# Denominators as jobs on a ring of three PSUM banks, Z in the staging tile, and the first batch's maxima and masks moved out of the opening pass

## What is computed

```python
xn = layernorm(x)
# A: 8 heads, latent attention; 32 latent dims each for queries, keys and a shared key part
c_q, c_kv, k_r = xn @ W_DQ + b_DQ, xn @ W_DKV + b_DKV, xn @ W_KR + b_KR
q = [c_q @ W_UQ + b_UQ, c_q @ W_QR + b_QR];  k = [c_kv @ W_UK + b_UK, k_r]
a = softmax(q @ k.T / sqrt(160)) @ (c_kv @ W_UV + b_UV) @ W_O + b_O
# B: 16 heads of 16 dims; every token's similarity to a guide vector, scaled by the
# minimum and maximum over ALL batches, gives pos = sim > 0.9; queries attend to keys of
# their own class and to 5 register keys; the 5 register queries see both classes
b = masked_attention(xn @ W_qkv, pos) @ W_proj + b_proj
out = x + a + b
```

## Time and profile before

| | us |
|---|---|
| median of three runs | 3077.69 |
| the profiled execution | 3083.09 |
| its span on the core | 3081.3 |
| PE busy (matmul) | 2900.2, 94% |
| DVE busy | 2256.7, 73% |
| ACT busy | 1676.5, 54% |
| POOL busy | 1428.3, 46% |

### The profile page before, as it was taken

The page is one execution under the profiler, slowest core; times in us unless marked ns, Lnnn a source line. Parts: engine busy times, 40 slices in busy tenths (PEclk is TensorE's granted clock), DMA queues, the critical chain, the costliest instruction groups (busy, mean ns, idle before and its releaser), DMA issues.

```text
span 3081.3 us, 45461 instructions
## 1 busy us (share of the span) xinstructions
PE 2900.2 (94%) x16898; PEld 1283.4 (42%) x16898; DVE 2256.7 (73%) x4085; ACT 1676.5 (54%) x1947; POOL 1428.3 (46%) x680
## 2 busy tenths in 40 slices
PE   5889999999999999999999999999999999999997
PEld 4634334443344443444334433444434443344433
DVE  5776787767877787767777677777787678776791
ACT  2424565544655566545565456555565456654574
POOL 6649522682227712285225832178122962258301
PEclk9979999998999999999999999999999999999998
DMA  4505234400352024411254003430145112540001
GB/s 148 180 16 98 69 86 99 82 16 30 105 100 62 19 74 97 107 27 34 68 110 89 16 31 92 102 74 20 53 101 114 31 37 63 117 92 16 17 17 36
DMA packets 128485, 211.43 MB, mean 69 GB/s; under 512 B 47560, under 2 KB 76136, under 8 KB 128120
## 3 DMA queue, kind: packets, MB, share of 16 engines
q1 hardware_dynamic: 124160, 201.10, 27.4%
q10 hardware_dynamic: 4104, 7.42, 0.6%
HBM read 136.21 MB, written 71.97 MB: 68 GB/s over the span
## 4 chain that ended last, share of the span: by engine, by line
PE 72%; DVE 13%; DMA 5%; POOL 4%; issue 3%; ACT 1%; SPq 1%; ACTq 0%; POOLq 0%; DVEq 0%
PE O L1207 20%; PE M L1108 12%; PE M L1102 10%; DVE mx L1448 10%; PE S L1192 7%; PE S L1195 6%; PE M L1128 3%; PE M L1172 2%; PE M L1174 2%; PE M L1221 2%; PE M L1140 2%; POOL PTx L734 2%; PE M L1146 1%; DMA recb_d<-RC 1%; DMA RB<-recb_d 1%
## 5 line engine op out<-in xcount | busy, mean ns | idle before, releaser
L1448 DVE TENSOR_REDUCE mx<-M 128x1 f32<-128x512 f32 x3072 | 1972.4, 683 | 567.9 <-PE M L1108 311.2
L956 ACT ACTIVATE PT<-S 128x1024 f32<-128x1024 f32 x1280 | 1241.9, 1022 | 818.5 <-PE S L1195 514.6
L1108 PE MATMUL M<-KB,QB 50*128 50x512 f32 x2048 | 671.3, 480 | 49.2 <-ACT stg L993 14.3
L1108 PEld LDWEIGHTS M<-KB,QB 50*128 50x128 f32 x2048 | 279.9, 185 | 691.6 <-DVE mx L1448 428.4
L1207 PE MATMUL O<-PT,VB 128*32 128x512 f32 x4096 | 554.6, 613 | 0.8 <-ACT PT L956 0.7
L1102 PE MATMUL M<-KA,QA 98*128 98x512 f32 x1024 | 433.0, 469 | 27.1 <-DVE mx L1448 22.0
L1195 PE MATMUL S<-QB,KB 52*128 52x512 f32 x2048 | 380.2, 434 | 6.2 <-DMA QB<-sh_d 2.3
L956 ACT ACTIVATE PTx<-S 128x1024 f32<-128x1024 f32 x256 | 250.2, 1023 | 228.2 <-PE S L1192 218.5
L1102 PEld LDWEIGHTS M<-KA,QA 98*128 98x128 f32 x1024 | 175.6, 191 | 348.8 <-DVE mx L1448 171.4
L1192 PE MATMUL S<-QA,KA 114*128 114x512 f32 x1024 | 316.0, 410 | 0.6 <-DMA QA<-sh_d 0.6
L788 POOL TENSOR_TENSOR PT<-PT,PTx 128x2048 f32<-128x2048 f32 x64 | 292.4, 4568 | 24.0 <-POOL PT L788 13.2
(11 more groups left out here) (153 smaller groups left out, 2120.0 us busy)
## 6 DMA issues: line engine op xcount, KB each, us to landing
qk_d<-stg SPq DMA_DIRECT2D x32, 1024.0 KB
KA<-kt_d SPq DMA_DIRECT2D x48, 512.0 KB, 7.3
QB<-qk_d SPq DMA_DIRECT2D x192, 128.0 KB
KB<-qk_d SPq DMA_DIRECT2D x192, 128.0 KB
kt_d<-stg SPq DMA_DIRECT2D x16, 1024.0 KB
RB<-recb_d SPq DMA_DIRECT2D x64, 256.0 KB
PT<-in_x SPq DMA_DIRECT2D x8, 1024.0 KB, 5.5
RB<-rec_d SPq DMA_DIRECT2D x32, 256.0 KB
```

Source lines behind the costliest of these rows:

```text
L956: nc.scalar.activation(probs(kind, of_a)[:, 2 * pair:2 * pair + 2, :], Sg[pair][:, :].rearrange("p (j s) -> p j s", j=2), ACT.Exp, scale=S ...
L1108: done = mm(m[:, :], QB[rows, 2 * q + a, at:at + P], KB[rows, 2 * q + a, keys], start=True, stop=True)
L1448: v.tensor_reduce(mx[:, g % 2, unit, kh:kh + 1], m[:, :], AX.X, ALU.max).then_inc(free, 1)
```

## The change

- `denominators`, `take_dens` and the semaphores of DN go. Job `dn` takes the same place in PE's order (first after `values` at steps 6, 10, ... 30 of A and step 2 of B), but writes to the next bank of the ring, each quad by itself. DVE copies the even quad's bank to half a tile in SBUF (latT, 128 x 512) and adds the odd quad's bank to it. SP stores from there.
- The ring has three banks in all of A and B.
- Z moves from PTx's memory to the staging tile `stg`. From batch 1 on POOL clears it at the head of A's stage, once the last fill of the batch is stored, and SP copies the register queries in during A's first group, after `load_b(n, 3)`. For batch 0 both stay in B's first group. The clearing grows from 1152 to 2048 columns.
- Fill `kb` (A's bias rows) goes. Its 8 rows are computed as 8 more latent columns: `Wlat` has 104 columns, made once at the start by three small matmuls, and `cq` is split and stored with 104 rows. `kt0` moves from B's step 18 to 20, `kt1` from 28 to 26.
- Opening pass: only the maxima of A's group 0 stay in it. Those of group 1 go to the first steps of batch 0's A, which now carries 160 units in 32 steps (7 a step, then 5, then 4 to 6). The extremes over partitions are found with a transpose, a DVE maximum and two small DMAs, in place of POOL's reduction. They, the marks and the masks' transposes are jobs of A's steps 1 to 6. POOL's fills of KA and KB and ACT's eight DMAs go. SP loads the selector rows and the ones from DRAM, and waits once for a DRAM to DRAM copy of them before it loads x of batch 2.

```diff
-FILLS = ("cq", "kt0", "kb", "kt1", "qk0", "qk1", "qk2", "qk3")
+FILLS = ("cq", "kt0", "kt1", "qk0", "qk1", "qk2", "qk3")
@@ prep_jobs
-    ma = max_units("a", 0) + max_units("a", 1)
-    out = [[] for _ in range(4 * B + 2)]
+    ma = max_units("a", 0)
+    out = [[] for _ in range(4 * B)]
     out[9] = [("va", 0)]
-    out[11] = fill_jobs("kb")
-    out[15] = fill_jobs("kt1")
-    for i in range(15):
-        out[17 + i] = ma[2 * i:2 * i + 2]
-    out[4 * B] = ma[30:32] + [("fa", "a", 0)] + ma[32:42]
-    out[4 * B + 1] = ma[42:]
+    out[11] = fill_jobs("kt1")
+    for i in range(16):
+        out[15 + i] += ma[2 * i:2 * i + 2]
+    out[31] += [("fa", "a", 0)]
+FIRST_MAXIMA = (7,) * 4 + (5,) * 12 + (4,) * 2 + (6, 4, 4, 6, 4, 4, 6, 4, 4, 4, 6, 4, 4, 4)
@@ jobs_b
+    s[2][2].insert(0, ("dn", QUADS - 1))
@@ jobs_a
     if first:
+        s[1][1].append(("ext",))
+        s[6][1].append(("mask",))
+    for i in range(QUADS - 1):
+        s[4 * i + 6][2].insert(0, ("dn", i))
@@
-def banks(slots, three):
+def banks(slots):
+    return [(j, 3) for step in slots for part in step for j in part]
@@ sync: a_steps, b_steps
                     if g == 0:
                         freed(b, 3)
                         load_b(n, 3)
+                        load_z(n)
...
                 if g == 0:
-                    load_z(b)
+                    if b == 0:
+                        load_z(b)
@@ gpsimd
         def clear_z(b):
-            wait_apart(pool, dn_done, b * QUADS + QUADS)
-            nc.gpsimd.memset(Z[:, 0:2 * QB_ * 144].bitcast(F32), 0.0).then_inc(z_clear, 1)
+            wait_apart(pool, st_out, stored(b, NF))
+            nc.gpsimd.memset(Z.bitcast(F32), 0.0).then_inc(z_clear, 1)
         def a_steps(n, b, before):
+            if before:
+                clear_z(n)
@@ scalar: exps
-                    act.wait_ge(dn_done, n * QUADS + i)
+                    spot = dn_spot(n, i - 1)
+                    act.wait_ge(m_full[spot.bank], spot.upto())
@@ tensor: job
+            elif kind == "dn":
+                pe.wait_ge(summed, n * ADDS + 3 * (j[1] + 1))
+                for jj in range(4):
+                    done = mm(m[32 * jj:32 * jj + 32, :], ones32[:, :], probs("a", 4 * j[1])[:, jj, :],
+                              start=True, stop=True, skip_group_check=True)
@@ vector: job
+            elif kind == "dn":
+                g, odd = j[1] // 2, j[1] % 2
+                to = DN[:, g % 2, :]
+                if odd:
+                    even = dn_spot(n, j[1] - 1)
+                    dve.wait_ge(m_free[even.bank], even.upto())
+                    v.tensor_tensor(to, m[:, :], to, ALU.add).then_inc(free, 1)
+                else:
+                    if g >= 2:
+                        dve.wait_ge(den_out, (n * GROUPS + g - 1) * 16)
+                    v.tensor_copy(to, m[:, :]).then_inc(free, 1)
             elif kind == "rs":
+                    dve.wait_ge(den_out, (n * GROUPS + GA) * 16)
```

More of the change, by code:

```diff
@@ L90, in place, with place_first @@
             step[2] = [u2, u3] + step[2]
+FIRST_MAXIMA = (7,) * 4 + (5,) * 12 + (4,) * 2 + (6, 4, 4, 6, 4, 4, 6, 4, 4, 4, 6, 4, 4, 4)
+def place_first(s):
+    units = iter(max_units("a", 1) + max_units("a", 2) + max_units("a", 3) + max_units("b", 0) + max_units("b", 1))
+    for step, n in zip(s, FIRST_MAXIMA):
+        us = list(itertools.islice(units, n))
+        front = 3 if n == 7 else 2
+        if us[0][0] == "ma":
+            step[0] += us[0:1]
+            step[2] = us[front:front + 1] + step[1] + step[2] + us[front + 1:]
+            step[1] = us[1:front]
+        else:
+            step[2] = us[n - 2:] + step[1] + step[2]
+            step[1] = us[0:n - 2]
 def jobs_b(more):
@@ L135, in jobs_a @@
             s[at][1].append(("po", 4 + c))
-    for g in range(GA):
+    if first:
+        place_first(s)
+    for g in (() if first else range(GA)):
         if g + 2 < GA:
@@ L140, in jobs_a @@
             place(s, g * NC, "b", g + 2 - GA)
-    return s
-def banks(slots, three):
-    out = []
-    for k, step in enumerate(slots):
-        out += [(j, 3 if three is not None and k >= three else 2) for part in step for j in part]
-    return out
+    for i in range(QUADS - 1):
+        s[4 * i + 6][2].insert(0, ("dn", i))
+    return s
+def banks(slots):
+    return [(j, 3) for step in slots for part in step for j in part]
 def index(jobs, used=(0, 0, 0)):
@@ L335, in program @@
     mask_f = take(2 * P).rearrange("p (s c) -> p s c", s=2)
-    one_row = take(S)
     zero = take(16)
     NH = B * NC * HB
-    n2, dots, root, newton = [take(NH) for _ in range(4)]
+    n2, dots, root = [take(NH) for _ in range(3)]
+    newton = take(NC * HB)
     xnT2 = take(2 * KD * S).rearrange("p (i k s) -> p i k s", i=2, k=KD)
@@ L641, in a_steps @@
                 kind, nxt = ("a", g + 1) if g + 1 < GA else ("b", 0)
+                if not before and g == 0:
+                    leave_extremes()
                 shift(n, kind, nxt, a_spot(n, b, ("fa", kind, nxt)))
@@ L1109, in job @@
                               start=True, stop=True)
+            elif kind == "ext":
+                pe.wait_ge(ext_ready, 1)
+                done = nc.tensor.transpose(m[0:2, 0:P], small[:, 0:2], ident[:, :])
+            elif kind == "mask":
+                pe.wait_ge(mask_ready, 1)
+                for f in range(2):
+                    done = nc.tensor.transpose(m[:, f * P:(f + 1) * P], masks[:, f, :, :].rearrange("p w c -> p (w c)"),
+                                               ident[:, :])
             elif kind == "fa":
@@ L1122, in job @@
                 pe.wait_ge(m_free[lat.bank], lat.upto())
[L1123 to L1124 removed]
+                lhs = Gk[:, 4 * int(kind[2]):4 * int(kind[2]) + 4, :].rearrange("p h i -> p (h i)")
+                done = mm(m[:, :], lhs, latT[0:LAT + 1, hf * HALF:(hf + 1) * HALF], start=True, stop=True)
             elif kind[:2] == "qk":
@@ L1209, in values @@
             last.then_inc(pv_done, 1)
-        def denominators(n, b, i):
-            g, c = i // 2, i % 2
-            if c == 0:
-                if g == 0 and b is not None:
-                    pe.wait_ge(m_free[2], b * LOOP[2] + U_B[2])
-                elif not (g == 0 and b is None):
-                    pe.wait_ge(dn_free, n * GA + g)
-            pe.wait_ge(summed, n * ADDS + 3 * (i + 1))
-            for jj in range(4):
-                last = mm(DN[32 * jj:32 * jj + 32, :], ones32[:, :], probs("a", 4 * i)[:, jj, :],
-                          start=(c == 0), stop=(c == 1), skip_group_check=True)
-            last.then_inc(dn_done, 1)
         def of_batch(j, n, b):
-            own = j[0] in ("mb", "rs", "rt", "rv", "po") or (j[0] == "fa" and j[1] == "b")
+            own = j[0] in ("mb", "dn", "rs", "rt", "rv", "po") or (j[0] == "fa" and j[1] == "b")
             return b if own else n
@@ L1272, in a_steps @@
                     values(b, STEPS_B - 1, "b")
-                if k >= 6 and k % 4 == 2:
-                    denominators(n, b, (k - 6) // 4)
                 some(k, 2)
@@ L1558, in a_steps @@
             for k in range(STEPS_A):
+                if not before and k == 5:
+                    marks()
                 for j in (j for part in slots[k] for j in part):
```

240 lines of the change are left out of this document (121 added, 119 removed).

## The result

The changed kernel takes **2926.69 us** (median of four runs, 2925.61 to 2931.60), the kernel before 3079.61 us beside it (four runs): a ratio of 0.951, 95% interval 0.949 to 0.954. The forecast was 2930. The profiled execution took 2925.61, and its span is 2923.8 us, against 3081.3.

What follows compares the result with a forecast made beforehand. PE, stalled 11.9 us by bank waits, was taken to bound A, DVE to pace B, and DVE's reductions to delay the opening's tail. 3083.1 - 36 + 3 - 51 - 40 - 28 = 2931; predicted 2930, range 2890 to 2995.

Steps and rivals of the forecast that it cites:

- part 1: A, batches 1 to 7: three banks shorten each stage from 129.8 to 122.5 us, 51 us in all (17 to 83).
- part 2: B's first group, eight batches: Z loaded a stage earlier and three banks gain 5.0 us each, 40 in all (16 to 56).
- a margin for POOL's last sum: B's first group: allowance for POOL's last addition, taking the group's estimate from 26.2 to 28.2 us.
- part 3: B's fourth group, seven batches: dropping kb gains 4.0 us each, 28 in all (7 to 33).
- part 4: Opening pass: fills and DMA issues go (7 us), extremes found sooner; A's first scores come 37 us earlier, 36 taken.
- part 5: Batch 0's A: 32 more units against bank waits saved give 147.6 us, 3 more than before (bounds 135 and 160).
- Three engines above 85% don't interleave without loss: Batch 0's A: reason for placing it at 147.6 us, with PE at 137, DVE 125.5 and POOL 120.9.
- (a): Rival: POOL takes PE's place in A, A stays near 127 and B begins 2 us late: 2979 us; chance 0.2.
- (b): Rival: only stops named by own rows (Z, kb, opening) go, banks bring little, A 127.3: 2988 us; chance 0.08.
- (e): Rival: PE's 0.60 between units is the row groups' price, not a bank wait, A stays at 129: 2996 us; chance 0.04.
- (c): Rival: cold stretches all vanish and A reaches its PE time of 118 to 119: 2893 us; chance 0.12.
- (d): Rival: POOL's additions hold DVE's 64 new denominator evictions 3.1 us each, making the kernel slower: 3129 us; chance 0.03.

Runs made afterwards that it cites:

- experiment 4: Changed kernel with GpSimd's additions over the first 256 of 512 columns only (and 1e-20 added in the even quads' copy): 2900.83 us, ratio 0.943.
- experiment 1: Changed kernel with two banks in A, not three (denominators stay jobs, B keeps three): 3038.87 us, ratio 0.988.
- experiment 9: Changed kernel with the last quad's denominators in B's step 3 in place of step 2: 2912.04 us, ratio 0.947.
- experiment 2: Changed kernel with two banks in B's steps 0 to 3 only: 2934.12 us, ratio 0.954.
- experiment 10: Changed kernel with SyncE's order edited in batch 0's A, Z cleared and loaded in B's first group, last quad's denominators in B's step 3: 2933.05 us, ratio 0.953.
- experiment 5: Kernel before the change with kt1's two jobs one step later (steps 29 and 30): 3059.59 us, ratio 0.994.
- Experiment 6: Changed kernel with a GpSimd fill of 32 partitions x 8192 put back between its first two normalisations: 2929.24 us, ratio 0.952.
- experiment 7: Changed kernel, SyncE in batch 0's A sending group 0's denominators and group 2's shift ahead of load_b(0, 1): 2913.55 us, ratio 0.948.
- run 16: Not a follow-up run: part of "PE had run 16 small ones", meaning PE had executed 16 small matmuls there; no time of its own.
- experiment 12: The kernel of experiment 10 with kt0's jobs back in B's step 18: 2940.39 us, ratio 0.955.
- experiment 3: Changed kernel with Z cleared and loaded in B's first group for all batches, in place of A's: 2921.99 us, ratio 0.950.

## Why the prediction came out right, and where its steps didn't

**What bounds A** (part 1) was read right and priced low. The 11.9 us of bank waits were all of it: PE alone is 118.0 (experiment 4) against 117.9, and the 32 pairs whose late starts made up 7.9 of them now lose 0.5. The step that failed is the placement at 122.5, "between PE's 118 and today's". I had added 4.6 us for POOL's chain and for quads of uneven length; it is 1.0. DVE was put too high as well, 97.8 us busy with eight denominators, where seven lie in A and it is 93.9. POOL's list ended even later than I had it (1010.9 - 882.4 = 128.5 us after the start, not 124; the pauses of 0.27 between additions, 16 of them, are 4.3 of that), and PE wants the last sum 8.6 us into B, so that POOL's floor for A is 128.5 - 8.6 = 120: A at 119.0 and PE's hold of 1.14 in B sit on it. Two limits 1 to 2 us apart, and the stage costs no more than the larger one: 3.5 x 7 = 24.5 us of error come from this one margin. The other side of the same sum is in experiment 1: the third bank is worth 15.9, of which the denominators as jobs eat 5.1 (I had counted their PE time as unchanged and left out that they queue).

**The clearing of Z** was expected at nothing, and is nothing: 0.95 us, with POOL idle for 8.83 ahead of it and for 5.52 behind it. Its duration, 1.9, had been worked out for 2048 columns; it has 1024.

**B's first group** (part 2): 3.8 us in place of 5.0 each (30.1 in place of 40). 28.2 is what it takes when PE isn't held (28.4 in batches 1 to 7, experiment 9). The failed term is "a margin for POOL's last sum", of which 1.3 more was needed: A became shorter, POOL's chain did not, and its end moved from 6.3 to 9.6 us into B, past step 2. Of my two reasons, banks and Z, the bank in steps 0 to 3 is worth 0.7 in batches 1 to 7 (experiment 2), and Z 4.2, but only without the hold (experiments 9 and 10).

**`kb`** (part 3): 4.8 in place of 4.0 a batch. The jobs' 1.7 was right, as far as a difference shows it; the wait and its aftermath are 3.1, not 2.3, since I had taken the best batch's 26.4 as free of it, and even that has 1.1 (25.3 in experiment 5).

**The opening** (part 4): -35.4 against -36. Experiment 6 measures the fill at 7.3, where I took 7, with the scatter of a few us told there; DVE's small instruction is held for nearly as long as the fill runs, 6706 and 6726 ns.

**Batch 0's A** (part 5) is the step that was wrong in kind: +12.7, not +3. "Three engines above 85% don't interleave without loss" had no row behind it, and DVE wasn't above 85%: it is busy for 113.2 us (experiment 7 has the same), not for 125.5, 72% of the stage. The loss is in SyncE's queue, which the prediction had walked through for the steady batches but not for this one: the kernel before has the two bulk loads and the store between them ahead of the shift as well, and the round trip in front of it took 8.9 there (256.85 to 265.73); but the shift went out at 266.18, 71.6 us into the stage, and its scores waited only 0.6 us for it:

```profile
266.18 0.37 SPq L533 DMA_DIRECT2D sh_d<-sh  x1
```

The change put `leave_extremes` and `leave_mask` ahead of them (the masks' stores, and a load of KB that SyncE waits 10.3 us for), so that the loads of `load_b(0, 0)` began 52 us into the stage, where it had been 37, and the shift went out 84.5 us into it, with step 16's scores due at 79. With two calls moved the stage is 147.8. That this is also the number I gave, 147.6, is luck: PE is busy for 139 of it and DVE for 113, not for the 137 and 125.5 that I had.

**The third groups**, +6.8, weren't in the sum. In five batches they take 26.8 to 27.8 in place of 25.4. In batch 2 (the changed kernel, view by windows, last columns PEclk, DMA share, GB/s):

```profile
1059.90:1065.00 5.10, 5.01 (x36) 3.19 (x36) 4.14 (x9) 2.54 (x3) 2.35 (x3) 1.00 0.04 5
1065.00:1070.00 5.00, 5.00 (x21) 1.69 (x17) 3.09 (x7) 2.78 (x3) 1.27 (x1) 0.52 0.50 142
1070.00:1075.00 5.00, 4.92 (x27) 1.52 (x28) 3.71 (x6) 3.04 (x4) 0.00 (x0) 0.80 0.23 71
1075.00:1080.00 5.00, 4.93 (x30) 1.89 (x30) 3.90 (x8) 2.89 (x4) 0.19 (x1) 1.00 0.04 8
```

The granted clock is 0.52 for 5 us (the level of 1.2 GHz) and then 1.00 again, and PE was busy for 5.01 of the 5.10 us before: no stop precedes it that a row shows. Among its usual matmuls PE had run 16 small ones there:

```profile
1062.51 1.97 PE L1175 MATMUL M<-ident,latT 96*128 96x32 f32 x16
```

The trace of experiment 9 has the same work there at 1.00 throughout. `kt0`'s place doesn't decide it (experiment 12), and banks and Z leave one to three such batches (experiments 1 to 3). These are counts from one execution of each kernel. What lowers it stays open.

**The rivals.** (a) POOL in PE's place: the sign that I had named for it came, 13.8 us of ACT's waits for POOL a stage against a limit of 10, but the sign was badly chosen, as nearly all of that wait is hidden behind PE. The price is 1.0 us a stage in A, not 4.5, and 1.3 to 1.4 in B's first group, not 2: its mechanism exists, at well under half of its price. (b) falls with A's 119.0, (e) with experiment 1. (c) Its A at 118 to 119, PE's own time, came true; its cold stretches did not all vanish, and none was in a steady A, where the clock was 1.00 before and is 1.00 now. The rule of the Trainium skill's page "TensorE: Matmul & The Clock Gate" (A second HAM failure mode: psum-queue depth-cycling) has no term here; nor does experiment 1's A show it, with two banks, 31 us of waits and a granted clock of 1.00. (d) is dead: all 64 evictions of denominators lie at 0.69 us, the 49 that run beside one of POOL's additions too, and the 17 of these that read an input from SBUF as well. That agrees with the Trainium skill's page "SBUF — State Buffer" (Who interferes with whom) for the additions. For copies that section makes a hold depend on conditions for their operands; the prediction's 99 us for them took these as met, and these copies, out of PSUM, weren't held either.

**Two better versions** came out: experiment 7 (2913.55) and experiment 9 (2912.04). Their edits touch different stages, so what both give together can be estimated from their stage lengths: 2923.8 - 9.5 - 5.5 (the first groups' sum in experiment 9, batch 0's longer one included) = 2909 us of span, and 2900 if the third groups' 8.5 come as well. That kernel wasn't run, and experiment 10 warns of such sums.

**The range.** The bounds "half way to its ends", 2905 to 2962, don't come out of the parts: added up, the halves give about 2897 to 2981. The measured time lies in either.

## What to carry to other kernels

When a stage's pacemaker is busy for 98% but its records overlap, count the waits in its merged timeline: the 11.9 us of them gave the length that PE alone allows within 0.1 (118.0 with POOL out of the way, 119.0 with it), and the margin added for the next engine was the error. Time that another engine waits isn't a price: 13.8 us of ACT's waits were worth 1.0. A wait can be hidden by another one, so undoing one edit proves only that it isn't needed beside the rest; test the pair. And for each stage that the change touches, walk the DMA queue in order, the first batch's as well as a steady one's: 16 DMAs of bulk loads in front of a 1.8 us round trip made it 6.9.

## What the runs showed of the hardware

A fill of 32 x 8192 on GpSimd (6.92 us) holds a VectorE instruction of 0.17 us for 6.71 and 6.73 in two kernels, while GpSimd's additions of 128 x 2048 don't lengthen VectorE's copies or additions from PSUM at all (690 to 693 ns in all 64, of which 49 ran beside one). A DMA of 8 KB that held its queue for 1.8 us with no load just ahead of it took 6.9 behind 16 loads from the same queue. And the granted clock fell to 0.52 for about 5 us inside a stretch in which PE was 98% busy or more.
